# Layer norms moved inside the programs that use them, and the zero rows written one program later, in a nine-stage vision tower

## The reference, cut to what matters

```python
def _layernorm(x, axis=-1, eps=1e-05):
    m = jnp.mean(x, axis=axis, keepdims=True)
    v = jnp.var(x, axis=axis, keepdims=True)
    return (x - m) / jnp.sqrt(v + eps)

h = _L0_tok_ref(x, L0_tok_W, L0_tok_b)
h = h + _L0_attn_ref(_layernorm(h), ...)   # softmax attention
h = h + _L0_ffn_ref(_layernorm(h), ...)    # 16 experts, top 2, and a shared expert
h = h + _L1_attn_ref(_layernorm(h), ...)   # linear attention
h = h + _L1_ffn_ref(_layernorm(h), ...)    # a block of its own: router, 12 heads, MLP, low rank
h = h + _L2_attn_ref(_layernorm(h), ...)   # selective scan
h = h + _L2_ffn_ref(_layernorm(h), ...)    # 128 experts, top 6, and a shared expert
h = h + _L3_attn_ref(_layernorm(h), ...)   # attention, 12 heads, sparse
h = h + _L3_ffn_ref(_layernorm(h), ...)    # 16 experts, top 3
```

## Time and profile before

| | |
|---|---|
| median of 3 runs | 971.91 us (962.59, 971.91, 974.63) |
| the profiled execution | 976.49 us, span of its trace 974.7 us |
| PE busy | 851.1 us (87%), 6279 records |
| PE weight loads busy | 683.1 us (70%) |
| DVE, ACT, POOL busy | 394.3, 303.5, 294.3 us (40%, 31%, 30%) |
| mean granted TensorE clock | 0.905 of full speed |

### The profile page before, as it was taken

The page is one execution under the profiler, slowest core; times in us unless marked ns, Lnnn a source line. Parts: engine busy times, 40 slices in busy tenths (PEclk is TensorE's granted clock), DMA queues, the critical chain, the costliest instruction groups (busy, mean ns, idle before and its releaser), DMA issues. The chain is left out here.

```text
span 974.7 us, 18786 instructions
## 1 busy us (share of the span) xinstructions
PE 851.1 (87%) x6279; PEld 683.1 (70%) x6279; DVE 394.3 (40%) x1187; ACT 303.5 (31%) x633; POOL 294.3 (30%) x316
## 2 busy tenths in 40 slices
PE   5997999798998886999978999999799959888881
PEld 4674889556575545999646999999555747678881
DVE  1335222214352025888483222222142793544443
ACT  1322122222444116675310222222124223324340
POOL 0002455200103105776023444444201000236672
PEclk9787899978878977999989999999899789789996
DMA  9515699600000033220053888998824200648985
GB/s 357 191 49 195 193 295 295 177 1 1 1 1 1 1 121 104 71 77 12 12 208 97 292 298 294 321 309 293 252 59 137 81 28 18 178 136 270 263 266 154
DMA packets 56444, 148.85 MB, mean 153 GB/s; under 512 B 7952, under 2 KB 18944, under 8 KB 55872
## 3 DMA queue, kind: packets, MB, share of 16 engines
q1 hardware_dynamic: 47296, 125.10, 38.8%
q0 software_dynamic: 9088, 22.98, 8.4%
HBM read 134.58 MB, written 13.47 MB: 152 GB/s over the span
## 5 line engine op out<-in xcount | busy, mean ns | idle before, releaser
L1459 POOL DMA_INDIRECT L_xr<-x_rows_L,L_rows_in x92 | 92.9, 1010 | 40.2 <-issue 33.5
L2250 DVE TENSOR_TENSOR L_act<-L_hid,bank 116x512 f32<-116x512 f32 (+1 forms) x56 | 35.8, 640 | 162.4 <-ACT L_hid L2219 115.0
L2139 POOL DMA_INDIRECT y_rows_L<-L_yb,L_rows_out x56 | 55.6, 993 | 108.6 <-ACT L_yb L2225 99.0
L2219 ACT ACTIVATE L_hid<-bank 116x512 f32<-116x512 f32 (+1 forms) x56 | 31.3, 559 | 166.3 <-PE bank L2189 147.1
L2183 PE MATMUL bank<-L_xtb,L_w 128*116 128x128 f32 (+1 forms) x464 | 58.7, 281 | 0.0
L2183 PEld LDWEIGHTS bank<-L_xtb,L_w 128*116 128x116 f32 (+1 forms) x464 | 56.0, 190 | 0.1
L2199 PE MATMUL bank<-L_w,L_act 116*128 116x192 f32 (+1 forms) x232 | 46.0, 339 | 2.6 <-ACT L_yb L2225 2.0
L140 ACT ACT_TABLE_LOAD x18 | 23.1, 1283 | 80.1 <-PEq L145 73.5
L1525 POOL TENSOR_TENSOR L_s_up<-L_s_hid,L_s_up 116x288 f32<-116x288 f32 (+1 forms) x10 | 7.9, 794 | 125.6 <-ACT L_s_up L1519 125.6
L1368 POOL TENSOR_TENSOR ssm_w_low<-ssm_wbc,ssm_w_high 128x512 fp32r<-128x512 f32 x24 | 31.4, 1310 | 44.6 <-ACT ssm_w_high L1327 44.6
L249 PE MATMUL bank<-par_const 128*128 128x512 f32 x62 | 41.4, 766 | 2.9 <-DVE L_xtb L2472 2.9
(11 more groups left out here) (462 smaller groups left out, 1881.5 us busy)
## 6 DMA issues: line engine op xcount, KB each, us to landing
L_w<-in_L2w SPq DMA_DIRECT2D x20, 696.0 KB
L_more<-in_L2w SPq DMA_DIRECT2D x20, 696.0 KB
L_w<-in_L2w SPq DMA_DIRECT2D x20, 384.0 KB
L_more<-in_L2w SPq DMA_DIRECT2D x20, 384.0 KB
L_w<-in_L0w SPq DMA_DIRECT2D x12, 576.0 KB
L_more<-in_L0w SPq DMA_DIRECT2D x12, 576.0 KB
ssm_wbc<-in_wBC SPq DMA_DIRECT2D x24, 256.0 KB
L_w<-in_L3w SPq DMA_DIRECT2D x16, 384.0 KB
```

The source lines that it names most:

```text
L1459: pool.indirect_dma_start(self.xr[j][:, :], None, self.x_rows[:, :], bass.IndirectOffsetOnAxis(ap=at, axis=0))\
L2139: pool.indirect_dma_start(X.y_rows[:, :], bass.IndirectOffsetOnAxis(ap=rows_out[h][:, j:j + 1], axis=0), y[s + j][:, :], None).then_inc(st ...
L2250: dve.tensor_tensor(act_out[j][:, :, :], hid[j][:, :, :], cols(up_bank[j % 2][0:N, 0:C * R], C), ALU.mult)\
```

## The change

`layer_norm` is no program any more. A class `Norm` holds its tensors and semaphores and has three methods, `pe`, `dve` and `act`, with the same instructions in the same order. Each user calls them as the first part of its own engine lists, and its first products wait for the normalized tokens (or for the affine result) by halves. `LN_WARM` goes from (1, 1) to (1, 0), so the matmul of `wake` after the spreading is gone at all nine places. Nine of the programs are gone with it. The waits for parameter groups move into the users. The nine DMAs that write zeros move from `load_all` to SP's list in the L0a attention. In `load_all`, DVE writes ones to a part of `xn` first, and PE multiplies them once (128 x 512) before its first wait for patches.

In three places other work keeps or gets a place beside the norm: in `selective_scan` SP's first tile loads and ACT's first two splits stand ahead of the norm, and the loads of the shared expert's weights stand after the second tile's; in `head_projections` POOL's clearing of `v` starts with the norm; in L3f DVE's `common.centre` stands after the norm. In L0f and L2f the norm's scratch tensors lie in two weight buffers that are loaded later.

```diff
-LN_WARM = (1, 1)
+LN_WARM = (1, 0)
...
         @block.sync
         def _(sp):
...
-            sp.wait_ge(zero_ready, 1)
-            for k, m in MOE.items():
-                sp.dma_start(T.x_rows[k][0:TILE, :], T.zero[0:TILE, 0:256 + m["experts"]]).then_inc(T.zeroed, 16)
-            rows = T.y_rows["L2"][8 * TILE:SPARE, :].rearrange("(i p k) d -> p i (k d)", p=TILE, k=8)
-            for i in range(TILES):
-                sp.dma_start(rows[:, i, 0:6 * DIM], T.zero[0:TILE, 0:6 * DIM]).then_inc(T.zeroed, 16)
             sp.wait_ge(T.loaded["const"], 16)
         @block.vector
         def _(dve):
-            dve.memset(T.zero[:, :], 0.0).then_inc(zero_ready, 1)
+            dve.memset(T.xn[:, 0, 0:512], 1.0).then_inc(ones_set, 1)
+            dve.memset(T.zero[:, :], 0.0)
...
         @block.tensor
         def _(pe):
+            pe.wait_ge(ones_set, 1)
+            pe.matmul(T.bank[7][:, :], T.xn[:, 0, 0:128], T.xn[:, 0, 0:512], start=True, stop=True)
             for k in range(PATCH_K):
...
-def layer_norm(T, name, x, out, meanwhile=None, on_pool=None, affine=(), func=None, again=None):
+class Norm:
...
+    def pe(self, pe):
+        T, HT, mean = self.T, TILES // 2, cols(self.T.p["mean192"], 2)
+        for s in range(2):
+            for c in range(2):
+                mm = pe.matmul(T.bank[s][:, 0:HALF], mean[:, c, :], self.x[:, c, HALF * s:HALF * s + HALF],
+                               start=(c == 0), stop=(c == 1))
+            mm.then_inc(self.means, 1)
+        wake(T, T.bank[6], LN_WARM[0])
...
+        wake(T, T.bank[7], LN_WARM[1])
...
+    def act(self, act):
+        T, HT, xc = self.T, TILES // 2, self.xc
+        T.load_table(ACT.Sqrt)
+        for s in range(2):
+            at = slice(HALF * s, HALF * s + HALF)
+            act.wait_ge(self.centred, s + 1)
+            act.activation(self.sq[:, :, at], xc[:, :, at], ACT.Square).then_inc(self.squared, 1)
...
+        for y, gb in self.affine:
...
+                ins.then_inc(self.affine_in, 1)
...
@@ def linear
+            if norm:
+                norm.pe(pe)
             if planes:
...
+                            if norm and u < 2 and k == 0:
+                                pe.wait_ge(norm.affine_in, u + 1)
...
@@ def wide_layer
+        @block.sync
+        def _(sp):
+            first_loads(sp)
+
         @block.tensor
         def _(pe):
+            norm.pe(pe)
+            pe.wait_ge(T.loaded[of_norm], 16)
             for s in range(2):
+                pe.wait_ge(norm.normalized, s + 1)
...
@@ def head_projections
-                                if router:
-                                    pe.wait_ge(router.xa_in, s + 1)
+                                if m == 0:
+                                    pe.wait_ge(router.xa_in if router else norm.normalized, s + 1)
...
+            norm.pe(pe)
             if router:
                 router.first(pe)
...
@@ class Router, first(pe)
+                if k == 0:
+                    pe.wait_ge(self.norm.affine_in, s + 1)
...
@@ def layer0_attention
+    def first_loads(sp):
+        for k, m in MOE.items():
+            sp.dma_start(T.x_rows[k][0:TILE, :], T.zero[0:TILE, 0:256 + m["experts"]]).then_inc(T.zeroed, 16)
+        rows = T.y_rows["L2"][8 * TILE:SPARE, :].rearrange("(i p k) d -> p i (k d)", p=TILE, k=8)
+        for i in range(TILES):
+            sp.dma_start(rows[:, i, 0:6 * DIM], T.zero[0:TILE, 0:6 * DIM]).then_inc(T.zeroed, 16)
+        for g in GROUPS:
+            if g not in ("tok", "const"):
+                sp.wait_ge(T.loaded[g], 16)
...
@@ def selective_scan
                 sp.dma_start(wbc[t % NW][:, :], T.dram["wBC"][t, :, :]).then_inc(loaded[t % NW], 16)
+                if t == 1:
+                    for to, name in zip(T.shared_L2, ("L2s1", "L2s2")):
+                        sp.dma_start(to, T.dram[name]).then_inc(T.shared_in["L2"], 16)
...
             split_high(0)
             split_high(1)
+            norm.act(act)
             for m in range(2):
                 act.wait_ge(pre_made, m + 1)
...
@@ def route
         @block.tensor
         def _(pe):
+            norm.pe(pe)
             for g in range(2):
+                pe.wait_ge(norm.normalized, g + 1)
```

More of the change, by code:

```diff
@@ L392, in linear @@
-def linear(T, name, outs, terms, lhsT, rhs, by_act=None, by_dve=None, size=Q, after=None, on_pool=None, planes=False, bridge=0):
+                act.wait_ge(self.normalized, s + 1)
+                for c in range(2):
+                    ins = act.activation(y[:, c, at], (self.out if self.again is None else self.again)[:, c, at], ACT.Identity,
+                                         bias=gb[:, 2 + c:3 + c], scale=gb[:, c:c + 1])
+                ins.then_inc(self.affine_in, 1)
+def linear(T, name, outs, terms, lhsT, rhs, by_act=None, by_dve=None, size=Q, after=None, on_pool=None, planes=False, bridge=0, norm=None):
@@ L1161, in layer1_block @@
             yr = sb("yr", [128, 2, TOKENS])
-            layer_norm(T, "b1_ln", T.h, x, lambda sp: sp.wait_ge(T.loaded["L1f"], 16),
-                       affine=[(yr, p["rln"])], func=ACT.Gelu, again=y)
             qk = sb("qk", [128, 4, TOKENS])
@@ L1259, in selective_scan @@
         wd = cols(T.full["sD"], 2)
+        norm = Norm(T, "L2a_ln", T.h, xs, ctx, (relu, mag), func=ACT.Exp)
         block = ctx.enter_context(nc.Block())
@@ L1277, in _ @@
                     for s in range(2):
+                        if m == 0 and k == 0:
+                            pe.wait_ge(norm.normalized, s + 1)
                         lanes = half_of(s) if k else slice(0, 128)
@@ L2540, in layer3_attention @@
         wide, second = sb("wide", [128, 2, IMAGES, 3, SEQ]), SecondWeights(T, ctx)
-        head_projections(T, "a3_proj", T.xn, w, cols(T.full["av"], 2), qk, p["aqkb"], v, wide, None, second)
+        norm = Norm(T, "L3a_ln", T.h, T.xn, ctx, func=ACT.Exp)
+        head_projections(T, "a3_proj", norm, T.xn, w, cols(T.full["av"], 2), qk, p["aqkb"], v, wide, None, second)
         head_attention(T, "a3_att", qk, wide, v, p["avb"], att, True, second)
@@ L2591, in build @@
             if s in plain:
-                def meanwhile(sp):
-                    sp.wait_ge(T.loaded[s], 16)
-                    if s == "L2a":
-                        for to, name in zip(T.shared_L2, ("L2s1", "L2s2")):
-                            sp.dma_start(to, T.dram[name]).then_inc(T.shared_in["L2"], 16)
-                if s != "L1f":
-                    layer_norm(T, f"{s}_ln", T.h, T.xn, meanwhile,
-                               func=ACT.Exp if s in ("L0a", "L2a", "L3a") else None)
                 plain[s](T)
```

249 lines of the change are left out of this document (113 added, 136 removed).

## The result

The changed kernel takes 962.69 us (median of 20 runs, 956.15 to 966.54); the kernel before took 972.22 us in 20 runs beside it (961.58 to 976.52). The ratio of their times is 0.993, 95% interval 0.9904 to 0.9956. (The ratios in this document leave out each kernel's slower runs, of which the kernel before has more, so they show a smaller gain than the medians: 0.993 is 6.8 us, the medians differ by 9.5 us, a ratio of 0.990.) Forecast were a median of 956, a gain of 15.6, and a range of 944 to 966. So the direction and the range held, and the size did not: the gain is 44% of the forecast by the ratio and 61% by the medians.

A forecast was written before the change was run, and what follows sets the result against it. PE, busy 87% of the span but much at half speed, was taken to bound the kernel, losing time at program seams. Terms summed to 19.1 us, less 3.5 for the clock: 15.6 off 971.9, 956.3; range 944 to 966.

The forecast's parts named there:

- Token products: First stretch: a matmul of ones while PE waits for patches speeds the slow first passes; 0.9 us, bounds 0 to 1.8.
- Zero writes: First program: without SP's zero writes the next program starts at 19.76 instead of 23.42; 3.7 us, bounds 3 to 4.
- the cover in L0a: The moved zero writes, over 11 us of issue on SP, fit within the L0a stage, which ended at 58.47.
- Norm of L0a: From L0a's first norm matmul to first product, 11.35 falls to 6.6: 4.7 us, 2 from the seam, 2.7 from the clock.
- Seams: Between norm and user's products, first products start at half 0: 1.8 L0f, 1.9 L1a and L3a, 1.0 L2f, 0.8 L3f.
- L2a: Splits ahead of the norm delay its end by 2.2 us, absorbed by the step sizes: counted 0, bounds -1.5 and +1.
- the rival with "L2a at its bad end": The start keeps its slow clock, 0.9 and 2.7 us missing: 961, or 962 with L2a's load landing late; chance 0.20.
- L2f: At L2f's norm, the first logits no longer wait for a wake and a program end: 1.0 us gained.
- The last rival: At nine norms, missing wakes leave another low clock stretch, 31 us lost less 15.6 gained: 987 us; chance 0.04.
- Clock give-back: Freed time filled at half rate: 1 us off at L0a, L1a and L3a, 0.5 for the others; 3.5, bounds 0 and 6.
- the signs named ahead: Right: `h` at 17 to 18.6, first norm at 18 to 20, L2a's square after 5.5 to 6.5; wrong: 0.45 token passes.
- the rival "everything pays": Whole kernel: the full 19.1, the rest of the token products and shorter low stretches, about 22 us, 950; chance 0.22.

The follow-up runs named there:

- the control: The changed kernel itself, run again unchanged in the second group: 953.46 us against 962.58 for the kernel before, ratio 0.9915.

## Why the prediction was right in direction and wrong in size

*Token products, 0.9 forecast:* nothing. Without the ones the time is the same, and the products took 14.91 and 14.57 with them, 14.33 without. The first passes stay slow with and without that matmul (7 and 8 passes in the 3.5 us from 4.5 on, 8 in the kernel before). The low end of the range (0) was right; the value between the ends wasn't.

*Zero writes, 3.7:* 2.7 in the profile of the changed kernel (of which the token products took 1.3 the other way), 3.3 in the control, 3.7 when moved alone. Right, and the cover in L0a held.

*Norm of L0a, 4.7:* 11.35 to 6.68 is 4.67, and the stage is 4.9 shorter. Right as a sum. But its parts aren't what the text made them: moving the writes alone brings 4.2 in L0a, so beside that the seam adds some 0.8, not 2, and with the writes back L0a is just as short. The norm's full clock did go with the missing idle time behind SP (2.18 against 3.65 for its first matmuls), but the stage as a whole gained nothing by it: the low stretch moved from the norm to the first products.

*Seams:* from the norm's first matmul to the user's first product the traces give 1.87 less in L0f (1.8 forecast), 2.73 in L1a (1.9, its low clock gone as well), 7.65 - 6.59 = 1.06 in L2f (1.0), 8.56 - 6.59 = 1.97 in L3a (1.9), 7.64 - 6.59 = 1.05 in L3f (0.8), 9.34 - 7.89 = 1.45 at the MLP's norm (1.2) and 0.5 in the L1 block (1.2; its norm fell into a low stretch). Reading a seam from where half 0 is ready was right nearly everywhere, to some tenths. The subtraction is not held by POOL: 0.76 and 0.75 beside it in L3a. The Trainium skill, "SBUF — State Buffer", section "Who interferes with whom", says that a VectorE instruction with at most one SBUF input, outside the two-port modes, does not contend with GpSimd; the trace agrees. DVE's L1056 takes 0.42 four times, so the collision of the earlier trace rows is gone.

*L2a, 0 (at worst -1.5 to +1):* **this is the step that failed.** The stage got 3.2 longer, and `delta` 5.3 later from the norm's start. The arithmetic of the halt was close: the first square was forecast 6.0 after the start and came 5.4 after it. But the text let the norm end only 2.2 later and then gave PE the durations of the kernel before (3.75 for the products). Half 0 was there 12.35 after the norm's start instead of 7.95, which is 4.4 later: the clock fell behind PE's idle 3.08 us, and L286, L292 and then the products took 1.9, 1.25 and 3 more. The slack that the text counted on, ACT busy with its splits, was there but small: from the end of PE's products to the end of the last step size it took 371.43 - 369.46 = 1.97 in the kernel before and 360.10 - 359.32 = 0.78 in the changed one. That covers 1.2 us of a delay of 6.5, and 5.3 are left. With the splits behind the norm L2a is 109.8, so the change could have brought 4.6 where it cost 3.2. That PE would fall to half speed behind its own wait is in none of the terms; the rival with "L2a at its bad end" had 1 us for the stage.

*L2f, 1.0:* the seam paid it, and then the logits lost 3.4 (8.11 against 4.69), and the stage is 3.0 longer. The last rival, low stretches behind the norm for want of a wake, named this mechanism and gave it 0.04 for nine places. It is real in L2f, and in L3f for the logits. "Real products of the same density start where the wake stood" was the argument against it; in L2f they did start there, at half speed, and with a wake of 1.05 in that place they ran at full speed in five kernels of five. In L3f the logits took 4.21 instead of 3.28, and are slower in all eight kernels without the wake there; that place was not tried by itself.

*Clock give-back, 3.5:* not measured by itself. The fit over runs puts 2.7 us on the lower mean clock, but at equal clock it leaves a gain of 11.8 and not the 19.1 of the sum, so it doesn't confirm the term. Its places were right in part: the first products of L0a and L1a did run partly at the low clock (both 0.79; L1a's took 8.19, and 6.55 in a kernel that gave them 1.00), those of L3a ran at 1.00. The larger losses lay in L2a, L2f and at the end of L1a, where the text had little or nothing.

Taken together: the two terms L2a (+3.2 instead of 0) and L2f (+3.0 instead of -1.0) are 7.2 us, and the median missed the forecast by 962.7 - 956.3 = 6.4. That the two numbers are so near is partly luck: the profiled executions differ by 11.0 where 15.6 were forecast, a miss of 4.6, so the other stages gained 2.6 more than their terms, the L1 block alone falling short by 2.6 (+1.4 instead of -1.2), and that surplus has no experiment behind it. Of the signs named ahead, `h` was complete at 19.95 and not by 18.6, the first norm started at 20.68 and not by 20, the first square of L2a came 5.4 and not 5.5 to 6.5 after the start, and the slow token passes, a sign of wrong, were there.

With both places mended the kernel gains 24.7 us in its group (ratio 0.9763), in the region of the rival "everything pays" (22). That version, splits behind the norm and one wake in L2f, beats both kernels: a gain of 24.7 over the kernel before beside it (940.07 against 964.73), where the changed kernel has 9.1 and 9.5 (ratios 0.9915 and 0.993). The wake at all nine places beside the splits takes 940.28, no different.

## What to carry to other kernels

Where programs are merged, look at which engine starts the chain of the merged part (here ACT, for the squares), and keep everything that waits for a transfer behind it, however short: a halt of 3 us cost the stage nearly 8 (117.6 against 109.8), and PE fell to half speed at its end in every kernel that had it. Read the seam from the moment at which the first half is ready; that gave six of nine norms within 0.3 us. And don't take a warming matmul away at all places at once: cost and gain of it are set place by place, and the trace of one place (a norm at 1.00 followed by products at 0.54) shows where to try it. What it then gives the whole kernel is another question: in L2f the stage got 3.4 us shorter, and the two spans differ by 0.7.

## What was not expected of the hardware

- The granted clock falls while PE is nominally busy. In L2f PE is busy 5.68 of 6 us through the norm at 1.00, mostly with matmuls of one moving column and of 96, and the clock is at 0.54 over the next 15 us although PE is then busy 14.95 of them. A matmul of 512 columns between norm and logits went with full speed there in all seven kernels that had it, the logits were slow in all seven that did not, and a second such matmul ahead of the one-column ones did not help. The Trainium skill, "TensorE: Matmul & The Clock Gate", section "What's actually happening", says that the array is throttled by default and that activity releases it. These rows do not show what counts as activity, only that the profile's busy time alone did not bring the clock back in these 15 us.
- In the first microseconds the clock column reads 1.00, yet passes take about twice as long (7 or 8 of them in the first 3.5 us, and later 6 in one us), with and without 2.07 us of PE work ahead of them.
- One kernel's runs on one chip spread by 1.1% (949.53 to 960.1 for the control), and go with the mean clock of the run. The same kernel, profiled twice, has a stage that differs by up to 3.8 us (L0f, 135.8 and 132.0).
